# VectorE, not GpSimd, applies the reciprocal norm to rotated queries and keys, and the entries around it move

## The reference, cut to what matters

```python
# layer 0: 16 heads of 64
h = layernorm(x); q = h @ Wq; k = ctx @ Wk; v = ctx @ Wv
x = x + (softmax(q k^T) * 64 ** -0.5 @ v) @ Wo + bo
# layer 1: 16 heads of 32
q = rotate(rmsnorm(x) @ wq); k = rotate(ctx @ wk)
q = q / max(norm(q), 1e-12); k = k / max(norm(k), 1e-12)
x = x + (softmax(q k^T * sqrt(32)) @ v) @ wout
```

## Time and profile before

| what | value |
|---|---|
| time, median of 3 runs | 3077.3 us (3076.02 to 3078.24) |
| the profiled execution's own time | 3081.01 us |
| its span | 3079.2 us |
| mean granted TensorE clock | 0.994 |
| busy: TensorE, VectorE, ScalarE, GpSimd | 2979.8, 2223.8, 1394.3, 512.9 us |

### The profile page before, as it was taken

The page is one execution under the profiler, slowest core; times in us unless marked ns, Lnnn a source line. Parts: engine busy times, 40 slices in busy tenths (PEclk is TensorE's granted clock), DMA queues, the critical chain, the costliest instruction groups (busy, mean ns, idle before and its releaser), DMA issues.

```text
span 3079.2 us, 69663 instructions
## 1 busy us (share of the span) xinstructions
PE 2979.8 (97%) x30112; PEld 1502.1 (49%) x30112; DVE 2223.8 (72%) x2395; ACT 1394.3 (45%) x1497; POOL 512.9 (17%) x349
## 2 busy tenths in 40 slices
PE   7999999999999999999999999999999999999999
PEld 4544545553444454555444445455534445445553
DVE  4767666787676777688767676768876767676877
ACT  3434334656433333465643333346563333334565
POOL 1000102450100000353010000035301000004440
PEclk9999999999999999999999999999999999999999
DMA  3000101201110000020121000002012000100001
GB/s 118 23 24 23 30 19 27 61 22 43 51 51 23 26 26 20 23 64 19 43 65 36 26 24 26 27 17 64 22 40 81 22 24 24 30 26 18 26 17 40
DMA packets 176391, 107.06 MB, mean 35 GB/s; under 512 B 79452, under 2 KB 145116, under 8 KB 176088
## 3 DMA queue, kind: packets, MB, share of 16 engines
q1 hardware_dynamic: 176088, 102.59, 12.0%
HBM read 93.12 MB, written 9.42 MB: 33 GB/s over the span
## 4 chain that ended last, share of the span: by engine, by line
PE 87%; DVE 5%; DMA 2%; ACT 2%; issue 2%; POOL 1%; SPq 0%; DVEq 0%; ACTq 0%
PE o_acc L762 20%; PE scores L749 16%; PE work L789 13%; PE work L783 12%; PE work L832 11%; PE scores L726 4%; PE work L698 4%; PE work L821 3%; DVE acc L969 2%; ACT probs L896 1%; PE scores L743 1%; PE work L815 1%; PE work L843 1%; DVE tile_max L951 1%; DMA rows_dram<-sums 1%
## 5 line engine op out<-in xcount | busy, mean ns | idle before, releaser
L896 ACT ACTIVATE probs<-scores 128x1024 f32<-128x1024 f32 (+1 forms) x744 | 935.7, 1291 | 432.4 <-PE scores L749 431.0
L969 DVE TENSOR_TENSOR acc<-acc,probs 128x1024 f32<-128x1024 f32 (+1 forms) x576 | 934.4, 1622 | 37.8 <-ACT probs L896 12.0
L951 DVE TENSOR_REDUCE tile_max<-work 128x2 f32<-128x1024 f32 x500 | 611.6, 1223 | 436.0 <-PE work L698 434.2
L762 PE MATMUL o_acc<-probs,v_tok 128*64 128x512 f32 (+1 forms) x4096 | 772.7, 607 | 0.0
L832 PE MATMUL work<-wo,o_sum 128*32 128x512 f32 (+2 forms) x2032 | 363.5, 606 | 25.3 <-issue 19.5
L749 PE MATMUL scores<-q_high,k_high 64*128 64x512 f32 (+1 forms) x1952 | 371.0, 493 | 7.6 <-ACT probs L896 7.5
L762 PEld LDWEIGHTS o_acc<-probs,v_tok 128*64 128x64 f32 (+1 forms) x4096 | 165.0, 122 | 313.8 <-issue 304.6
L749 PE MATMUL scores<-q_low,k_high 64*128 64x512 f32 (+1 forms) x1952 | 296.4, 391 | 0.0
L749 PE MATMUL scores<-q_high,k_low 64*128 64x512 f32 (+1 forms) x1952 | 295.0, 390 | 0.0
L1096 POOL CAST neg_max<-neg 128x8 bf16<-128x8 f32 x64 | 20.1, 315 | 1641.2 <-DVE neg L956 1641.2
L789 PEld LDWEIGHTS work<-wv,cT 128*64 128x64 f32 (+2 forms) x6000 | 256.4, 124 | 56.9 <-issue 54.8
(11 more groups left out here) (87 smaller groups left out, 2607.1 us busy)
## 6 DMA issues: line engine op xcount, KB each, us to landing
recip<-rows_dram SPq DMA_DIRECT2D x128, 128.0 KB, 3.1
stage<-in_x_dram SPq DMA_DIRECT2D x8, 1024.0 KB, 6.9
wq<-in_L_xattn_Wq_dram SPq DMA_DIRECT2D x32, 256.0 KB, 2.8
resid<-in_x_dram SPq DMA_DIRECT2D x8, 1024.0 KB, 5.3
wo<-in_L_xattn_Wo_dram SPq DMA_DIRECT2D x32, 256.0 KB, 2.8
recip<-rows_dram SPq DMA_DIRECT2D x124, 64.0 KB, 2.1
out_dram<-resid SPq DMA_DIRECT2D x7, 1024.0 KB, 4.8
wk<-in_L_xattn_Wk_dram SPq DMA_DIRECT2D x32, 192.0 KB, 2.5
```

The costliest lines, as they stand in the source:

```text
L762: mm = pe.matmul(o_acc[h * d:(h + 1) * d, :], v_tok[par][:, kt, h * d:(h + 1) * d], probs[:, unit_slot(t, n, kt, h // 2), h % 2, :], start ...
L896: act.activation(block_probs(t, n, kt), scores[:, 2 * (no % 2):2 * (no % 2) + g, :], ACT.Exp, scale=(1.0, float(D1) ** 0.5 / QK_SCALE ** 2 ...
L951: dve.tensor_reduce(tile_max[:, qt, :, n:n + 1], maxima_banks(e), AX.X, ALU.max, negate=True).then_inc(dve_freed, 1)
L969: dve.tensor_tensor(a, block_probs(t, n, 0) if kt == 1 else a, block_probs(t, n, kt), ALU.add).then_inc(add_ok, units)
```

## The change

GpSimd keeps L1104 and L1106. Its multiplication L1109 goes; a new entry "scale", put at the end of the fill of the step after each rotation, lets VectorE do the same multiplication. It waits for GpSimd's sum. GpSimd in turn waits for the scale of two rotations before, ahead of L1104, since inv has two buffers. The bias is added in four instructions of one tile each in place of one. The maxima in layer 1's last two halves stand one to a step, from step 4 of (3,0) to step 7 of (3,1); before, steps 6 of (3,0) and 1 of (3,1) had two, steps 2 and 7 of (3,1) none. In layer 1, den of an even turn moves from the head to the end of step 1's fill (behind ct and load_c where they stand there); the outputs move from steps 5, 6, 7, 7 to steps 6, 6, 7, 7; one output in layer 0 moves behind a T.

```diff
-        ends = (0, 0, 0, 0, 0, 1, 2, 4, 5, 6, 8, 8, 9, 10, 11, 12, 12)
+        ends = (0, 0, 0, 0, 0, 1, 2, 3, 4, 5, 6, 7, 8, 9, 10, 11, 12)
...
-        beside[1][:0] = E("den", t, n)
+        if p % 2:
+            beside[1][:0] = E("den", t, n)
+        else:
+            beside[1] += E("den", t, n)
...
-            at = min(5 + i, 7)
+            at = 6 + i // 2
...
-                    beside[i] = E("out", t0, n0 * HT + 1 + i) + beside[i]
+                    at = 1 if (p, n, i) == (7, 0, 2) else 0
+                    beside[i][at:at] = E("out", t0, n0 * HT + 1 + i)
...
+    for st, after in zip(steps[::-1][1:], steps[::-1]):
+        after.fill += [Entry("scale", e.t, (e.kind, e.i)) for e in st.fill if e.kind in ("kr", "qr")]
...
+                elif e.kind == "scale":
+                    kind, half = e.i
+                    no = ITEM[kind, e.t, half].rope
+                    vec = raw["kq".index(kind[0])][:, tiles_of(half), :, :].rearrange("p t h d -> p (t h) d")
+                    dve.wait_ge(turn_step, 2 * no)
+                    dve.tensor_tensor(vec, vec, inv[no % 2][:, :].unsqueeze(2).broadcast_to([P, HT * G1, D1]), ALU.mult).then_inc(scaled_ok, 1)
...
                 pool.wait_ge(sumsq_ok, no)
+                if no > 2:
+                    pool.wait_ge(scaled_ok, no - 2)
                 pool.tensor_tensor(inv[no % 2][:, :], sumsq[no % 2][:, :], power[:, :], ALU.pow).then_inc(turn_step, 1)
                 pool.wait_ge(dve_freed, e.dve)
                 pool.tensor_tensor(vec, vec, turned[no % 2][:, :, :, :], ALU.add).then_inc(turn_step, 1)
-                pool.wait_ge(turn_step, 2 * no)
-                vec = vec.rearrange("p t h d -> p (t h) d")
-                pool.tensor_tensor(vec, vec, inv[no % 2][:, :].unsqueeze(2).broadcast_to([P, HT * G1, D1]), ALU.mult).then_inc(scaled_ok, 1)
...
-                pool.tensor_tensor(resid[:, ts, :], resid[:, ts, :], bo_all[:, :].unsqueeze(1).broadcast_to([P, HT, D]), ALU.add).then_inc(bias_ok, 1)
+                for i in range(half * HT, half * HT + HT):
+                    added = pool.tensor_tensor(resid[:, i, :], resid[:, i, :], bo_all[:, :], ALU.add)
+                added.then_inc(bias_ok, 1)
```

## The result

The changed kernel took 3092.87 us (median of 6 runs, 3088.74 to 3099.87) against 3077.77 us of the kernel before beside it (6 runs, 3073.93 to 3082.50): a ratio of 1.0054, 95% interval [1.0039, 1.0068], so 12 to 21 us slower. Forecast was slower, 3086 us, own range 3084 to 3099. The profiled execution took 3089.58 us, its span is 3087.8 us, 8.6 us longer than before's. The granted clock is 0.994 in both.

The account below looks back on a forecast made before the run. TensorE, busy for 97% of the span, was taken to bound the kernel by its work and waits. Losses of 24.3 us less gains of 15.2 put 9.1 on 3077.3: 3086 us, own range 3084 to 3099, 8-in-10 range 3059 to 3099.

Parts of the forecast that it names:

- (0,1): First pair's output in this half: TensorE waits 4.7 us, before 2.64; 1.7 us lost a batch, 8.5 us in all.
- VectorE's lateness at L975: In (0,1), up to L975: 0.7, 3.7 and 1.7 us, less 0.8 of stalls that go, 5.3 us late.
- Rival 1: VectorE late by less than the outputs' 3.6 us move, so output waits vanish: 3045 us, or 3061 with half; chance 0.15.
- (2,0): Output of the second pair's half: waits of 3.0 us against 0.9, 2.1 lost in three batches, 0.5 in the last: 6.8 us.
- The two claims: In (2,0), TensorE's claims of the rotation's bank and of kT's bank would wait about 0.4 us each.
- (0,0): Output at 557.06: one scale ahead of norm_o, 0.65 us lost four times, 2.6 us.
- Other rotations stand before idle time of VectorE: nothing: Rotations outside (0,1), (2,0) and (0,0): moving their product to VectorE would cost nothing.
- The maxima: In (3,0) and (3,1): TensorE waits 2.2 to 2.8 us at T; 6.4 us lost net with two half-rate stretches.
- den: Denominator behind the context loads: all 7.7 us of context-tile waits and one half-rate stretch go, 9.4 us gained.
- The output behind T: One output in layer 0 moved behind a T: costs and brings nothing, since TensorE works on either.
- The bias: Bias added in four: VectorE's two adds beside it 1.1 us better in each of two batches, 2.2 us gained.
- The end: Last half's first output: its 1.86 us wait for norm_o and its half rate go, 3.6 us gained.

Follow-up runs that it names:

- e1: The changed kernel with GpSimd multiplying again, so the new places and the bias in four alone: 3051.99 us, ratio 0.9919 to the kernel before.
- e4: The changed kernel with the product two steps behind the rotation where the next step is the first of a half: 3071.69 us, ratio 0.9984 to the kernel before.
- e12: The changed kernel with VectorE's product behind the maxima at a step's end, not ahead of them: 3083.66 us, ratio 1.0026 to the kernel before.
- e3: The changed kernel with the maxima at the places they had before: 3087.75 us, ratio 1.0034 to the kernel before.
- e5: The changed kernel with GpSimd multiplying again and the maxima at the places they had before: 3052.07 us, ratio 0.9911 to the kernel before.
- e8: The kernel before with only layer 1's outputs moved from steps 5, 6, 7, 7 to 6, 6, 7, 7: 3063.56 us, ratio 0.9946.
- e7: The kernel before with only the denominator of even turns moved to the end of step 1: 3071.54 us, ratio 0.9981.
- e9: The kernel before with only the one output of layer 0 moved behind T: 3071.51 us, ratio 0.9985.
- e6: The kernel before with only the bias added in four instructions of one tile: 3073.85 us, ratio 0.9988.

## Why the prediction was right or wrong

**The sign and the mechanism were right.** VectorE stands for 3.02 and 3.01 us at the starts of (0,1) and (2,0), ended by the sum; the product takes 0.69 us; the wait at T came with 2.90, 2.65 and 2.64 us; the waits for context tiles went; the adds beside the bias take 3.70 us. Undoing the product gives 41 us (e1), undoing only its idle time 21 us (e4). The size was 7 us short of the median. In the spans the sum is almost exact (+9.1 predicted, +8.6), but that is luck: its terms missed in both directions.

- *(0,1), +8.5 predicted, -0.2 measured.* The mis-sized term is VectorE's lateness at L975, put at 5.3 us. Against the earlier trace rows the first add starts 6.2 us later, of which TensorE's own 2.38 are taken off: 3.8, not 4.4. Then 1.7 for the second product, as predicted, less 0.8 of stalls; and that product (L981 in the changed kernel) took 1.16 us, not 1.76: 4.1 us. The second mistake: TensorE was to gain 0.5 us on the way (1.1 less 0.6), and gained nothing: (1,0) became 0.5 us longer. With both right, the step's own sum gives 2.64 + 4.1 - 3.6 = 3.1, and the trace has 3.04. Over four batches the waits are 10.4 us where they were 10.6. (By the prediction's own figures, too, the net is 4.7 - 2.64 - 0.5 = 1.6 us a batch, not 1.7.)
- *Rival 1* ("the lateness is absorbed") had its turning point wrong for the same step. Moving the outputs by 3.6 us leaves the wait that was there if VectorE is 3.6 us later; it vanishes only below 3.6 - 2.64 = 1.0 us of lateness. e4 and e1 are on that side.
- *(2,0), +6.8 predicted, +4.4.* The denominator's 0.8 us came as said. The two claims wait 0.1 and 0.24 us in place of 0.4 each. At the outputs the first waits 0, 0.66 and 0.64 us in the three batches and the second 0.83, for a bank, where 1.4 for norm_o was expected; and 0.5 us for ScalarE came in addition. Also misread was the state before: 0.92 us is the first batch's wait alone, the second's was 2.15. *(0,0)*: 1.58 for 1.04 us, 2.0 for 2.6.
- *"Other rotations stand before idle time of VectorE: nothing"* is the step that failed outright. Two places: in (6,1) of layer 0 the product stands ahead of a reduction that TensorE waits for, 1.90 us (the term is 8.1 us between e1 and the changed kernel, 9 us in e12); and in (1,0) the low part of qT is late for the scores, 1.00 us four times. The latter, with 0.5 us for ScalarE ahead of it, ate the gain from L1109's wait, which had been 1.1 us four times a few us earlier.
- *The maxima, +6.4 predicted, +5.6 measured.* As changed kernel against before, the parts are near: T waits 2.90, 2.65 and 2.64 us; the waits for the maxima fall from 2.6 us a batch to 0.8 (the one of 1.8 us that was to stay is not there, 0.76 us for ScalarE is); all waits of the stretch together are 1.1, 0.8 and 0.8 us longer; and three stretches behind T have a granted clock of 0.51 to 0.53, where two were counted. But it is not the price of the maxima's places. With the old places as much is lost (e3 5.9, e5 6.5), since *the outputs' move in (3,1)*, which the prediction never priced, brings waits of its own (e8: 5.2). A reader who undid the maxima on the strength of this term would gain nothing in this stretch.
- *den, -9.4 predicted, -4.2 measured* (e7 alone: 2.5 to 9.2 us gained). The context waits went, but den now claims the bank that the low part of qT leaves: 1.14 us, three times.
- *The output behind T, nothing predicted*: 4.6 us gained (e9). "TensorE works on either" overlooked that ScalarE's copy of T is waited for.
- *The bias, -2.2*: 2.3 us less waiting in e6, but 0.7 in the changed kernel, whose third place lost 0.7 us. *The end, -3.6*: -2.8.

The prediction weighed the Trainium skill's "SBUF — State Buffer", Who interferes with whom, at the bias: whoever starts first holds the shared ports for its whole instruction. From it the prediction worked out that short instructions let VectorE in between. The trace agrees: the pair of adds went from 5.00 to 3.60 and 3.70 us. GpSimd's burst itself grew from 4.58 to 6.94 us, by 2.36 us, about two adds of 1.2 us.

What the measured 12 to 21 us have beyond the 8.6 us of the spans is not settled. Single executions of the changed kernel scatter over 11 us (3088.74 to 3099.87) and of the kernel before over 9, and each column of the table is one of them.

## What to carry to other kernels

An instruction moved to another engine's in-order queue is priced by what it waits for and who stands behind it: here 44 us of work, for which the page shows 28% of idle time on its engine, cost 41 us, half of it where one entry stood idle 3 us in a step that had no other work. Split a change into its parts before judging it: these places gain 25 us and this product loses 44. And when a consumer is moved later by some time, subtract the wait that it had first: only what is left is room for a later producer.

## What the runs showed of the hardware

- The bias in four back-to-back GpSimd instructions of 128x512 took 6.94 us where one of 128x2048 took 4.58, in the changed kernel and in e6 alike, while VectorE's two adds ran among them.
- GpSimd's conversion of 128x8 elements took 2.24 us beside VectorE's add of 2.29 us that had begun 0.12 us before it, and 0.22 us at 870.95, beside a short reduction and a product. The subtraction behind the slow one took 0.54 us beside a product of 0.68 us, where the earlier trace rows have 2.36 beside an add. So the price of T's wait is the length of VectorE's instruction, not GpSimd's work.
- VectorE's product with the reciprocal norm broadcast over 32 columns took 688 ns for 128x512, as the plain product of the earlier trace rows; a 32nd of the columns still took 185 ns.
